# A graph layer and a top-1 mixture of experts on one core: the choice of the expert in two parts, the second layer's weight halves side by side, and the first routing rows loaded behind the border

## The chip, the core and the metric

The kernel runs on one core of a Trainium2 chip. TensorE (PE) multiplies matrices, VectorE (DVE), ScalarE (ACT) and GpSimd (POOL) work on rows in SBUF and on the banks (PSUM) that PE writes, and SyncE (SP) issues transfers. The metric is the device time of one execution in microseconds, lower is better.

## The reference

```python
x = x + graph_layer(layernorm(x), edges)         # 20000 rows of 256, 10000 edges
h = layernorm(x)
logits = h @ gate_w + gate_b                     # 8 experts
probs = softmax(logits); idx = argmax(probs)     # one expert for each row, ties to the first
kept = (rank of the row within its expert) < 3125   # at most 3125 rows each
hid = relu(h @ w1[idx] + b1[idx])                # 256 -> 1024
y = (hid @ w2[idx] + b2[idx]) * prob * kept      # 1024 -> 256
x = x + nan_to_num(y, posinf=1e4, neginf=-1e4)
```

In the graph layer each edge takes the normalised row of its sender, is weighted by a small network of its embedding (8 to 64 to 320) and by its direction, and is summed at its receiver. The sum goes through two 64x64 matrices and is added to the receiver's row. Everything is float32.

## The kernel before

The work is cut into four blocks of code, with a border (all engines wait for each other) between them. Each block has its own program for each engine, and the engines wait for one another by semaphores. The order within an engine is written out by hand.

**Edges and nodes, `edge_block`, 0 to 354 us.** There are 20 edge groups and 20 node chunks of eight tiles (40 transfers, 24 through `xin` and 16 through `shared`). The loop over steps g makes the radial weights (`ps_w`) and the messages of edge group g, and sums them per receiver (`ps_agg`, then the two matrices). ACT's order in a step is `rows_by_direction`, `take_agg`, `take_upd`, with the adding and storing of node chunks (`add_own_rows`, `store_rows`) woven in for the first STEPS = 10 steps. POOL gathers the senders' rows, works out scales (`node_scales`, `edge_scales`) and at the end adds the summed rows to DRAM (`scatter`). In the last steps, SP already loads the first four groups of new rows from `out` into `shared`, and DVE takes their layer statistics (`Early`, U = 4 buffers).

**Routing, `routing_block`, 354.8 to 527 us.** The 20480 rows (160 tiles of 128, the last few padding) go by in NG = 40 groups of four tiles. For each group PE turns the rows (16 transposes), ACT rounds them to a short format (`xt_hi`), DVE forms the rest (`xt_lo`, L1265) and, one group ahead, the statistics. PE then multiplies by the gate's weights and turns the logits back. POOL makes the coefficients of eight tiles (`coefs`) and the scaled logits (`scaled_logits`), 20 times each. After the last of them DVE chooses the expert of all 160 tiles in five operations from `best` (L1291) on:

```python
v.wait_ge(scaled_ready, NCO)
chain.link(red(best[:], logits[:], AX.X, ALU.max))
```

Then the places within each expert are counted, and tables of row numbers per expert are made.

**Experts, `expert_block`, 529 us to the end.** Rows of one expert are worked on in blocks, and each expert has some narrow blocks of two tiles first (its loop from `start` to `wide`), then wide ones of three tiles (from `wide` to `end`). Here there are 52 blocks, 14 narrow and 38 wide. A float32 product is made of three products of a short format: with a = a_hi + a_lo and b = b_hi + b_lo it is a_hi b_hi + a_lo b_hi + a_hi b_lo. For one block b:

- PE: the first layer (L1717) in eight parts f of 128 hidden units, six matmuls each over all the block's rows, into one of SLOTS = 4 banks `ps_h`. Then the second layer (L1729) in four parts j of two f each, for each tile and each f three matmuls of 256 columns into `ps_y`. After part 0 it turns the rows of block b + 1 into `ps_x` (L1707). The next f may start once the bank of f - 4 has been read (`h_taken`).
- ACT: the relu of each f twice, rounded (`h_hi`) and in full (`h_all`). Behind f == 1 it scales block b - 1's result by the probability (`scale_rows`, three activations), behind f == 3 it normalises the gathered rows of the block after next (`normalise`, L1641, 3 activations) and keeps their probabilities. Behind f == 7 it rounds the turned rows of b + 1 to `x_hi` (L1650). In the first wide block of an expert it also rounds four parts of the next expert's weights.
- DVE: `h_lo` in four parts, `x_lo`, the other four of the eight rounded weight parts and all eight low parts, `y_sum` (bank plus bias), and the clean-up of infinities.
- POOL: for b + 2 three pairs of gathers (`xg` L1462, `sg` L1468) also where the block has two tiles, then three adds of result rows into `out` (L1579). One loop runs over all blocks.
- SP: the loads of the next expert's weights.

The end, after the last block, scales and stores tile by tile (`scale_rows_end`, L1601), behind the whole second layer.

The rounded weights of both layers lie in one tile, the rest in another. The second layer's loop is, in short:

```python
for i in range(tiles):
    for f in (2 * j, 2 * j + 1):
        # h_hi x w_hi, h_lo x w_hi, h_hi x w_lo, 256 columns each
```

## Time and profile before

| | |
|---|---|
| median of 3 runs | 1412.29 us (1410.97 to 1415.54) |
| the profiled execution | 1410.77 us |
| its span, first to last instruction | 1408.9 us |
| busy: PE, DVE, ACT, POOL | 1213.6, 1001.1, 954.3, 1015.8 us |
| share of the span | 86%, 71%, 68%, 72% |
| mean granted clock of TensorE | 0.944 |

The busy times are those of one profiled execution. The share of an engine is an average over four stages with different limits, so the stages have to be read one by one. What a stretch waits for is seen in the chain that ended last, and in the bracket behind a row of the timeline: the idle time before that instruction, and what released it.

### The profile page before, as it was taken

What the parts mean: (1) busy time and instruction counts of PE and PEld (TensorE: products, weight loads), DVE (VectorE), ACT (ScalarE), POOL (GpSimd) and SP (SyncE); (2) the same over time, 40 slices, a digit from 0 to 9 for tenths busy, and PEclk for the clock granted to TensorE, in tenths of its full rate; (3) what the DMA queues carried; (4) which work ended last, traced back from release to release, by engine and by line L of the source; (5) the groups of instructions that cost most, each with busy time, mean ns of one, the idle gap of its engine ahead of it and who ended that gap; (6) DMA issues with size and microseconds to landing.
All of it is one profiled execution on the core that took longest, in us unless ns stands there. A gap on an engine that the chain in (4) does not pass through costs nothing.

```text
span 1408.9 us, 26705 instructions
## 1 busy us (share of the span) xinstructions
PE 1213.6 (86%) x7869; PEld 1067.7 (76%) x7870; DVE 1001.1 (71%) x2059; ACT 954.3 (68%) x2127; POOL 1015.8 (72%) x913
## 2 busy tenths in 40 slices
PE   2487578887998147999999999999999999999995
PEld 0244345555555137999999999999999999999995
DVE  7999998987898976657657555755755575556754
ACT  4789898885666256666667666766766776656673
POOL 7788878887788016767768767777776777678874
PEclk9977778999999588999999999999999999999998
DMA  9888996456776003433435323433423353333333
GB/s 336 235 269 280 289 213 163 70 85 110 218 219 225 9 8 98 109 45 46 109 46 114 50 45 46 109 47 50 109 45 45 49 114 47 45 46 53 54 54 40
DMA packets 131809, 153.01 MB, mean 109 GB/s; under 512 B 17218, under 2 KB 118658, under 8 KB 131606
## 3 DMA queue, kind: packets, MB, share of 16 engines
q0 software_dynamic: 51328, 64.07, 29.0%
q1 hardware_dynamic: 58758, 66.60, 14.7%
q10 hardware_dynamic: 21648, 21.49, 4.5%
q8 instruction: 29, 0.48, 0.1%
q14 instruction: 46, 0.38, 0.1%
HBM read 98.30 MB, written 53.81 MB: 108 GB/s over the span
## 4 chain that ended last, share of the span: by engine, by line
PE 57%; issue 2%; ACT 1%; POOL 1%; DMA 1%; DVE 1%; ACTq 0%; POOLq 0%; DVEq 0%
PE f_ps_y L1729 28%; PE f_ps_h L1717 26%; PE f_ps_x L1707 2%; DMA sg<-stat_rows,idx_now 1%; ACT y_all L1667 0%; ACT h_hi L1656 0%; ACT h_all L1657 0%; POOL xg L1462 0%; POOL sg L1468 0%; ACT f_xn L1641 0%; POOL out L1601 0%; DVE clean_end L1844 0%; DVE clean_end L1843 0%; ACT f_xn L1618 0%; DVE y_sum L1824 0%
## 5 line engine op out<-in xcount | busy, mean ns | idle before, releaser
L1656 ACT ACTIVATE h_hi<-f_ps_h,c_b 128x384 fp32r<-128x384 f32 (+1 forms) x416 | 236.4, 568 | 267.1 <-PE f_ps_h L1717 267.1
L1767 DVE TENSOR_TENSOR h_lo<-h_all,h_hi 128x768 fp32r<-128x768 f32 (+1 forms) x208 | 184.4, 886 | 258.3 <-ACT h_all L1657 257.1
L1729 PE MATMUL f_ps_y<-w_hi,h_hi 128*128 128x256 f32 x1136 | 325.4, 286 | 0.0
L1729 PE MATMUL f_ps_y<-w_hi,h_lo 128*128 128x256 f32 x1136 | 320.6, 282 | 0.0
L1729 PE MATMUL f_ps_y<-w_lo,h_hi 128*128 128x256 f32 x1136 | 319.1, 281 | 0.0
L1579 POOL DMA_INDIRECT out<-clean,put_now x156 | 255.8, 1640 | 56.7 <-issue 47.3
L1462 POOL DMA_INDIRECT xg<-out,idx_now x156 | 187.2, 1200 | 129.3 <-issue 120.6
L1717 PE MATMUL f_ps_h<-x_hi,w_hi 128*128 128x384 f32 (+1 forms) x832 | 271.3, 326 | 9.3 <-issue 3.4
L1717 PE MATMUL f_ps_h<-x_lo,w_hi 128*128 128x384 f32 (+1 forms) x832 | 268.6, 323 | 0.0
L1717 PE MATMUL f_ps_h<-x_hi,w_lo 128*128 128x384 f32 (+1 forms) x832 | 268.5, 323 | 0.0
L1657 ACT ACTIVATE h_all<-f_ps_h,c_b 128x384 f32<-128x384 f32 (+1 forms) x416 | 237.6, 571 | 0.0
L1468 POOL DMA_INDIRECT sg<-stat_rows,idx_now x156 | 189.7, 1216 | 47.9 <-issue 47.9
L1729 PEld LDWEIGHTS f_ps_y<-w_lo,h_hi 128*128 128x128 f32 x1136 | 215.3, 190 | 0.0
L1729 PEld LDWEIGHTS f_ps_y<-w_hi,h_hi 128*128 128x128 f32 x1136 | 213.3, 188 | 0.5 <-DVE h_lo L1767 0.3
L1729 PEld LDWEIGHTS f_ps_y<-w_hi,h_lo 128*128 128x128 f32 x1136 | 213.3, 188 | 0.0
L1717 PEld LDWEIGHTS f_ps_h<-x_hi,w_hi 128*128 128x128 f32 x832 | 157.7, 190 | 13.8 <-issue 8.4
L1717 PEld LDWEIGHTS f_ps_h<-x_lo,w_hi 128*128 128x128 f32 x832 | 157.9, 190 | 0.0
L1717 PEld LDWEIGHTS f_ps_h<-x_hi,w_lo 128*128 128x128 f32 x832 | 157.7, 190 | 0.0
L647 PEld LDWEIGHTS ps_agg<-same,msg 128*128 128x128 f32 x320 | 68.9, 233 | 66.2 <-issue 56.0
L647 PE MATMUL ps_agg<-same,msg 128*128 128x512 f32 (+3 forms) x320 | 114.6, 521 | 2.7 <-ACT late_rows L581 1.6
L636 PE MATMUL ps_w<-fc,hidden 64*128 64x320 f32 x160 | 59.8, 524 | 49.6 <-DVE tmp_h L808 48.8
L530 ACT ACTIVATE y<-y,edge_dir 128x256 f32<-128x256 f32 x240 | 100.0, 498 | 0.7
(245 smaller groups left out, 2260.8 us busy)
## 6 DMA issues: line engine op xcount, KB each, us to landing
shared<-out SPq DMA_DIRECT2D x40, 512.0 KB, 4.1
w_raw<-in_w SPq DMA_DIRECT2D x16, 1024.0 KB, 7.1
xin<-in_x SPq DMA_DIRECT2D x24, 512.0 KB, 7.2
out<-xin ACTq DMA_DIRECT2D x24, 512.0 KB, 5.5
shared<-in_x SPq DMA_DIRECT2D x16, 512.0 KB, 5.4
out<-shared ACTq DMA_DIRECT2D x16, 512.0 KB, 5.2
dst_row<-in_dst SPq DMA_DIRECT2D x20, 256.0 KB, 4.8
xg<-out,idx_now POOLq DMA_INDIRECT x156
```

Source lines behind the costliest of these rows:

```text
L530: ins = nc.scalar.activation(y[g % 2][:, t, 1 + i, :], y[g % 2][:, t, 0, :], ACT.Copy, scale=edge_dir[:, GT * g + t, i:i + 1])
L636: ins = nc.tensor.matmul(ps_w[:, t, :5 * MUL], hidden[:, t * P:(t + 1) * P], fc2[:], start=True, stop=True)
L647: ins = nc.tensor.matmul(ps_agg[:, c, t * P:], msg[g % 2][:, t].rearrange("p u j -> p (u j)")[:, c::2], same[g % 2][t][:], start=t == 0, s ...
L1462: return nc.gpsimd.indirect_dma_start(self.xg[:, i, :], None, self.out, bass.IndirectOffsetOnAxis(idx[:, i, 0:1].bitcast(U32), 0), bounds_ ...
L1468: return nc.gpsimd.indirect_dma_start(self.sg[:, i, :], None, self.stat_rows, bass.IndirectOffsetOnAxis(idx[:, i, 1:2].bitcast(U32), 0), b ...
L1579: nc.gpsimd.indirect_dma_start(out, bass.IndirectOffsetOnAxis(put_now[:, i:i + 1].bitcast(U32), 0), clean[:, i, :], None, bounds_check=ROW ...
L1656: nc.scalar.activation(h_hi[:, f, :n * P], ps_h[:, f % SLOTS, :n * P], ACT.Relu, bias=b1[:, e, f:f + 1])
L1657: nc.scalar.activation(h_all[f // 2 % 2][:, f % 2, :n * P], ps_h[:, f % SLOTS, :n * P], ACT.Relu, bias=b1[:, e, f:f + 1]).then_inc(h_taken, 1)
L1707: ins = nc.tensor.transpose(ps_x[:, c, i * P:(i + 1) * P], xn[:, i, c * P:(c + 1) * P], ident[:])
L1717: ins = nc.tensor.matmul(ps_h[:, f % SLOTS, :tiles * P], weights[s][:, w], x[:, c, :tiles * P], start=n == 0, stop=n == 5)
L1729: ins = nc.tensor.matmul(ps_y[:, i], x[:, f, i * P:(i + 1) * P], weights[s][:, w], start=i != 1 and f == 0 and n == 0, stop=f == KF - 1 an ...
L1767: tt(h_lo[:, pair, :n * P], h_all[j % 2][:, :, :n * P], h_hi[:, pair, :n * P].bitcast(F32), ALU.subtract).then_inc(h_lo_ready, 1)
```

## The change

- **Second layer.** The high and low halves of `w2` now lie side by side in one tile. `h_hi` is multiplied by both in one matmul of 512 columns, `h_lo` by the high half in one of 256. The bank `ps_y` is two halves wide for each tile (three banks), `ps_h` has three slots instead of four, and DVE adds both halves in two additions.
- **ACT and DVE.** Scaling by the probability moves from ACT to DVE. ACT rounds all weights (`AHEAD` = 6 parts before the relus, the rest behind `x_hi`), DVE forms only the low halves. `normalise` and `keep_prob` stand behind all eight relus. PE turns the next rows behind part 1 of the second layer instead of part 0.
- **POOL and SP.** POOL gathers two tiles for a narrow block; it has loops by expert for that, with a table `wide_blocks` that three more small DVE instructions make. SP waits for the gathers' landing and passes it on (`rows_in`), and issues the next expert's weight load at the start of each expert.
- **The last block** runs its second layer tile by tile, and DVE scales and cleans each tile as it is ready. The clearing of `y_sum` no longer stands before the first block.
- **The choice** of the expert is made for 144 tiles, once 18 of 20 parts of the logits are there, and then for the last 16.
- **Border.** `Early` goes: the first four groups are loaded after the border, SP's wait for the scatters written into the routing block, and their statistics are taken there.
- **Edge loop.** In ACT's program the adding of the last node chunk moves behind `rows_by_direction` and its store behind `take_upd`. The statistics of edge groups from 14 on are taken one step later and the coefficients of a step before its statistics. SP's loads of embeddings and receivers and POOL's `edge_scales` of one group come one place earlier.

```diff
+            next_receivers(STEPS - 1)
+            next_embedding(STEPS)
             for a in range(2):
                 sp.wait_ge(x1_out[(NC - 1) % RING][a], 16 * ((NC - 1) // RING + 1))
             sp.sem_inc(stored, 1)
-            next_receivers(STEPS - 1)
-            for g in range(STEPS, EG):
+            next_receivers(STEPS)
+            for g in range(STEPS + 1, EG):
...
-            for g in range(early.U):
-                early.load(sp, g)
...
-                if 2 * n - 2 < STEPS:
+                if 2 * n - 2 <= STEPS:
...
-                if g + 1 == STEPS:
-                    add_own_rows(2 * g + 1)
-                    store_rows(NC - 1, 1)
                 next_rows(g + 1)
                 rows_by_direction(g + 1, (0, 1))
                 take_agg(g - 1)
                 if g + 1 < STEPS:
                     add_own_rows(2 * g + 1)
                 rows_by_direction(g + 1, (2, 3))
+                if g + 1 == STEPS:
+                    add_own_rows(2 * g + 1)
                 take_upd(g - 1)
+            store_rows(NC - 1, 1)
...
-                return (n - 3) // 2 if n < STEPS else n - 6
+                if n >= SLOTS:
+                    return n - 5
+                return (n - 3) // 2 if n <= STEPS else n - 6
...
-            for g in range(U, NG):
-                sp.wait_ge(turned, g - U + 1)
-                sp.wait_ge(stats_ready, g - U + 1)
-                early.load(sp, g)
+            for g in range(NG):
+                if g >= U:
+                    sp.wait_ge(turned, g - U + 1)
+                    sp.wait_ge(stats_ready, g - U + 1)
+                if g % U == 0:
+                    needed = sp.value_load(writes.of_rows[0:1, g + U - 1:g + U], min_val=64,
+                                           max_val=32 * EG + 64)
+                    for h in range(2):
+                        sp.wait_ge(writes.scattered[h], needed)
+                        sp.sem_inc(spare_sp, 1)
+                sp.dma_start(rows[:, g % U], x1_v[g]).then_inc(rows_in[g % U], 16)
...
-            nc.vector.tensor_copy(stats[:, :U * GT], early.stats[:]).then_inc(stats_ready, U)
...
+            statistics(0)
             for g in range(NG):
-                if U <= g + 1 < NG:
-                    early.statistics(nc, v, g + 1, stats).then_inc(stats_ready, 1)
+                if g + 1 < NG:
+                    statistics(g + 1)
                 turned_half(g)
...
+            def choose(t):
+                n = t.stop - t.start
+                chain.link(red(best[:, t], logits[:, t], AX.X, ALU.max))
+                chain.link(tt(is_best[:, t], logits[:, t], over_experts(best[:, t]), ALU.is_equal))
+                chain.link(tt(score[:, t], is_best[:, t], falling_b[:].unsqueeze(1).broadcast_to([P, n, NEXP]), ALU.mult))
+                chain.link(red(first[:, t], score[:, t], AX.X, ALU.max))
+                chain.link(tt(chosen[:, t], score[:, t], over_experts(first[:, t]), ALU.is_equal))
+
+            LAST = 2 * CC
+            v.wait_ge(scaled_ready, NCO - 2)
+            choose(slice(0, NT - LAST))
             v.wait_ge(scaled_ready, NCO)
-            chain.link(red(best[:], logits[:], AX.X, ALU.max))
-            chain.link(tt(is_best[:], logits[:], over_experts(best[:]), ALU.is_equal))
-            chain.link(tt(score[:], is_best[:], over_tokens(falling_b), ALU.mult))
-            chain.link(red(first[:], score[:], AX.X, ALU.max))
-            chain.mark(tt(chosen[:], score[:], over_experts(first[:]), ALU.is_equal))
-            chain.wait()
+            choose(slice(NT - LAST, NT))
...
+            chain.mark(nc.vector.tensor_tensor_scan(wide_upto[:], ones_row[:, :NEXP], wide[:], 0.0, ALU.mult, ALU.add))
+            chain.mark(nc.vector.tensor_copy(wide_blocks[:, 0], wide[:1]))
+            chain.mark(tt(place[:], place[:], chosen[:], ALU.mult))
+            chain.wait(1)
+            chain.mark(stt(out=wide_blocks[:, 1], in0=wide_upto[:1], scalar=narrow[:1, 0:1], in1=wide[:1],
+                           op0=ALU.add, op1=ALU.subtract))
...
+        self.up_hi, self.up_lo, self.down = [], [], [[], []]
+        for n, up in enumerate((self.up_hi, self.up_hi, self.up_lo, self.up_lo)):
+            up.append(half(f"w_up{n}", [P, self.W1]))
+            self.down[n // 2].append(half(f"w_down{n}", [P, self.HALF, 2, D]))
...
-    SLOTS = 4
+    SLOTS = 3
+    AHEAD = 6
...
-        ps_y = ps("f_ps_y", [P, 4, D])
+        ps_y = ps("f_ps_y", [P, BT, 2, D])
...
+            def gather(b, tiles):
                 pool.wait_ge(idx_ready, b)
                 pool.sem_inc(spare_pool, 1)
-                for i in range(BT):
-                    gathers.rows(nc, idx_now, i).then_inc(gathered, 16)
-                    gathers.stats(nc, idx_now, i).then_inc(gathered, 16)
+                for i in range(tiles):
+                    landed = gathered if i < 2 else gathered_third
+                    gathers.rows(nc, idx_now, i).then_inc(landed, 16)
+                    gathers.stats(nc, idx_now, i).then_inc(landed, 16)
+
+            def step(b, tiles):
+                pool.wait_ge(xn_ready, b)
+                pool.wait_ge(prob_next_ready, b)
+                pool.sem_inc(spare_pool, 1)
+                gather(b, tiles)
+                add_rows(b - 3)
...
+                if split is not None:
+                    for c in range(AHEAD):
+                        weights.split_high(nc, act, e + 1, split, c)
...
-                    if f == 1:
-                        scale_rows(b - 1)
-                    if f == 3:
-                        act.wait_ge(turned, b + 1)
-                        act.sem_inc(spare_act, 1)
-                        normalise(b + 1)
-                        act.wait_ge(prob_ready, b + 2)
-                        act.sem_inc(spare_act, 1)
-                        keep_prob()
-                    if split is not None and f >= KF - BY_ACT:
-                        weights.split_high(nc, act, e + 1, split, f - (KF - BY_ACT))
+                act.wait_ge(turned, b + 1)
+                act.sem_inc(spare_act, 1)
+                normalise(b + 1)
+                act.wait_ge(prob_ready, b + 2)
+                act.sem_inc(spare_act, 1)
+                keep_prob()
                 take_high(b + 1)
+                if split is not None:
+                    for c in range(AHEAD, CUTS):
+                        weights.split_high(nc, act, e + 1, split, c)
...
-                pe.wait_ge(h_taken, KF * b + (f + 1))
+                pe.wait_ge(h_taken, KF * b + (f + 1 if f >= SLOTS else SLOTS))
...
+            def down(s, j, i):
+                for f in (2 * j, 2 * j + 1):
+                    w = w_down[s][f // HALF]
+                    nc.tensor.matmul(ps_y[:, i], h_hi[:, f, i * P:(i + 1) * P], w[:, f % HALF],
+                                     start=f == 0, stop=False)
+                    ins = nc.tensor.matmul(ps_y[:, i, 1], h_lo[:, f, i * P:(i + 1) * P], w[:, f % HALF, 0],
+                                           start=False, stop=f == KF - 1)
                 return ins
...
-                    if j == 0:
+                    hidden_ready(b, j)
+                    for i in range(tiles):
+                        ins = down(e % 2, j, i)
+                    if j == 1:
                         turn(b + 1)
                 ins.then_inc(y_ready, 1)
+
+            def last_step(e, b):
+                first_layer(e, b, BT)
+                for i in range(BT):
+                    for j in range(KJ):
+                        if i == 0:
+                            hidden_ready(b, j)
+                        ins = down(e % 2, j, i)
+                    ins.then_inc(y_tile_ready, 1)
...
+            def scale_rows(b):
+                v.wait_ge(y_sum_ready, b + 2)
+                v.wait_ge(prob_ready, b + 2)
+                v.wait_ge(clean_ready, b + 2)
+                v.sem_inc(spare_dve, 1)
+                tt(y_all[:], y_sum[:], prob[:].unsqueeze(2).broadcast_to([P, BT, D]), ALU.mult).then_inc(y_step, 2)
...
-                        for c in (2 * j, 2 * j + 1):
-                            if c < CUTS - BY_ACT:
-                                weights.split_own(nc, v, tt, e + 1, split, BY_ACT + c, (CUTS - BY_ACT) * e + c + 1)
-                            else:
-                                a = c - (CUTS - BY_ACT)
-                                weights.split_low(v, tt, e + 1, split, a, CUTS + BY_ACT * e + a + 1)
+                        for c in range(2 * j, min(2 * j + 2, AHEAD)):
+                            weights.split_low(v, tt, e + 1, split, c, CUTS * e + CUTS + c + 1)
...
-                tt(y_sum[:, :n], ps_y[:, :n], b2[:, bass.ds(e, 1)].broadcast_to([P, n, D]),
-                   ALU.add).then_inc(y_sum_ready, 1)
+                v.sem_inc(spare_dve, 1)
+                tt(y_sum[:, :n], ps_y[:, :n, 1], b2[:, bass.ds(e, 1)].broadcast_to([P, n, D]),
+                   ALU.add).then_inc(y_step, 1)
+                v.wait_ge(y_step, 3 * b + 3)
+                v.sem_inc(spare_dve, 1)
+                tt(y_sum[:, :n], ps_y[:, :n, 0], y_sum[:, :n], ALU.add).then_inc(y_sum_ready, 1)
...
+            add_infinities(last - 1)
+            keep_finite(last - 1)
+            nc.vector.tensor_copy(put_end[:], put_row[:, bass.ds(BT * last + 2 * BT, BT)])
+            v.wait_ge(prob_ready, last + 2)
+            v.wait_ge(clean_ready, last + 2)
+            v.sem_inc(spare_dve, 1)
             for i in range(BT):
-                v.wait_ge(y_end_ready, i + 1)
+                v.wait_ge(y_tile_ready, i + 1)
+                chain.link(tt(y_sum[:, i], ps_y[:, i, 1], b2[:, NEXP - 1], ALU.add))
+                chain.link(tt(y_sum[:, i], ps_y[:, i, 0], y_sum[:, i], ALU.add))
+                chain.link(ts(y_all[:, i], y_sum[:, i], prob[:, i:i + 1], None, ALU.mult))
```

## Rows read from the trace of the kernel before

**Rows 1.** Page part 4, the chain that ended last, by engine.

```profile
PE 57%; issue 2%; ACT 1%; POOL 1%; DMA 1%; DVE 1%; ACTq 0%; POOLq 0%; DVEq 0%
```

**Rows 2.** The chain in order of time, middle of the expert stage (start us, us, work).

```profile
587.35 8.33 PE f_ps_h L1717 x48
595.68 2.16 PE f_ps_y L1729 x18
...
598.50 6.47 PE f_ps_y L1729 x54
```

**Rows 3.** Table of stretches: busy us (instructions) of each engine, granted clock, DMA.

```profile
535.51:551.96 16.45, 15.36 (x103) 15.01 (x104) 6.11 (x11) 9.69 (x25) 7.26 (x8) 0.83 0.48 154
587.35:604.97 17.62, 17.62 (x127) 17.62 (x127) 9.38 (x13) 11.22 (x25) 12.86 (x10) 1.00 0.32 48
640.69:653.52 12.83, 12.64 (x103) 12.43 (x104) 7.15 (x13) 9.48 (x25) 8.62 (x7) 1.00 0.36 50
724.63:750.05 25.42, 25.00 (x205) 24.59 (x206) 14.68 (x25) 18.96 (x50) 18.73 (x15) 1.00 0.39 55
1256.38:1296.38 40.00, 38.06 (x307) 36.92 (x308) 22.51 (x38) 28.65 (x75) 30.59 (x23) 1.00 0.39 55
```

**Rows 4.** Timeline of PE in the routing block (start us, us, engine, line).

```profile
395.16 0.62 PE L1206 MATMUL banks<-xt_lo,r_gate_parts 128*8 128x512 f32 x2
395.62 0.60 PE L1193 MATMUL banks<-c_ident,shared 128*128 128x128 f32 x4
```

**Rows 5.** Timeline of ACT in the expert stage; brackets: idle before, releaser.

```profile
606.23 0.58 ACT L1656 ACTIVATE h_hi<-f_ps_h,c_b 128x384 fp32r<-128x384 f32 x1 [6.40 <-PE f_ps_h L1717]
...
611.28 1.61 ACT L1641 ACTIVATE f_xn<-xg,sg 128x256 f32<-128x256 f32 x3
...
616.57 0.87 ACT L1650 CAST x_hi<-f_ps_x 128x768 fp32r<-128x768 f32 x1
```

**Rows 6.** Timeline of POOL, same stretch.

```profile
596.38 1.09 POOL L1462 DMA_INDIRECT xg<-out,idx_now  x1 [2.27 <-issue]
...
605.74 1.63 POOL L1579 DMA_INDIRECT out<-clean,put_now  x1 [0.30 <-issue]
```

**Rows 7.** Timeline of POOL and ACT in the triple of narrow blocks.

```profile
1286.41 1.21 POOL L1468 DMA_INDIRECT sg<-stat_rows,idx_now  x1 [0.30 <-issue]
...
1289.21 0.20 ACT L1611 COPY idx_now<-idx_row 128x6 int32 x1 [2.06 <-DMA sg<-stat_rows,idx_now]
```

**Rows 8.** Timeline of ACT in the first expert block.

```profile
544.80 0.20 ACT L1611 COPY idx_now<-idx_row 128x6 int32 x1 [2.73 <-DMA sg<-stat_rows,idx_now]
```

**Rows 9.** The chain in order of time, the end.

```profile
1375.36 8.33 PE f_ps_h L1717 x48
...
1401.47 1.55 POOL out L1601
```

**Rows 10.** Timeline of DVE where the edge loop begins.

```profile
230.18 0.50 DVE L793 TENSOR_TENSOR tmp_d<-y 128x256 f32<-128x256 f32 x1 [5.61 <-PE ps_w L636]
```

**Rows 11.** Timeline of DVE and PE around the border (355 us).

```profile
342.83 5.31 DVE L157 BATCH_NORM_STATS2 early_stats<-shared 128x6 f32<-128x256 f32 x16
...
355.47 2.31 PEld L1193 LDWEIGHTS banks<-c_ident,shared 128*128 128x128 f32 x16
```

**Rows 12.** Page part 6, DMA issues: count, KB each, median us to landing.

```profile
shared<-out SPq DMA_DIRECT2D x40, 512.0 KB, 4.1
```

**Rows 13.** Timeline of DVE in routing and at the choice.

```profile
401.21 1.21 DVE L1265 TENSOR_TENSOR xt_lo<-banks,xt_hi 128x1024 fp32r<-128x1024 f32 x1
...
406.08 1.20 DVE L1265 TENSOR_TENSOR xt_lo<-banks,xt_hi 128x1024 fp32r<-128x1024 f32 x1
...
451.35 1.22 DVE L1265 TENSOR_TENSOR xt_lo<-banks,xt_hi 128x1024 fp32r<-128x1024 f32 x1 [0.21 <-ACT xt_hi L1147]
457.64 1.49 DVE L1291 TENSOR_REDUCE best<-logits 128x160 f32<-128x1280 f32 x1 [5.07 <-POOL logits L1112]
...
464.62 0.19 DVE L1297 TENSOR_TENSOR chosen<-chosen,c_valid 128x32 bf16<-128x32 bf16 x1
```

305 lines of the change are left out of this document (155 added, 150 removed).

## The prediction

> **What bounds the kernel now.** I read the page's chain first. TensorE carries 57% of it, nearly all in the two expert layers [rows 1]. So the next view is the chain in order of time in the middle of the expert stage. A block of three tiles costs 8.33 us for 48 first-layer matmuls, 2.16 and 6.47 us for 72 second-layer ones, and the rest of its 17.62 us is the turning of the next rows, 0.66 us [rows 2]. Nothing is idle in it. The table of stretches says the same: PE busy for 17.62 of 17.62 us, DVE 9.38, ACT 11.22, POOL 12.86, at a granted clock of 1.00 [rows 3]. Blocks of two tiles are different. Their PE work is 48 and 48 matmuls of 256 columns and one turn. At 6.47/54 = 0.1198 us each that is 11.50 + 0.66 = 12.16 us. They take 12.83 us alone, 25.42 as a pair, and 40.00 us as a triple [rows 3]. So a few tenths are lost in each and 3.5 us in the triple. There are 38 wide and 14 narrow blocks: one narrow at the start, two alone, four pairs, one triple. Before the expert stage stand the edge loop, where ACT, PE and DVE take turns, and routing, where DVE and POOL are both full.
>
> **The second layer.** Per tile and hidden chunk, three matmuls of 256 columns become one of 512 and one of 256. Columns are equal, instructions go from three to two. What is an instruction worth? 384 columns take 8.33/48 = 0.1735 us and 256 take 0.1198 [rows 2]. The difference, 0.0537 for 128 columns, is 0.42 ns each, which is the 2.4 GHz level, and leaves 0.1198 - 0.1074 = 12.4 ns that do not depend on columns. A 512-column matmul would then take 0.2272 us and replace 0.2396: 12.4 ns saved. The only fast-format 512-column matmuls in the trace are the gate's. Two of them start at 395.16 and the next work at 395.62, 0.23 us each [rows 4]. That is 10 ns saved, but their weights are 8 columns wide. The bounds are 0 (the row says nothing of 128 columns of weights; a loss has no reason, as the columns are the same) and 12.4. I take 12.4, since both shapes it is drawn from have this very weight load. With 24 merges in a wide block that is 0.30 us, over 37 blocks 11.1 us (the last one is counted at the end). A narrow block has 16, 0.20 us.
>
> The Trainium skill (TensorE: Matmul & The Clock Gate, "Wait — 56ns, not 53.3ns?") gives the warm spacing as columns over 2.4 GHz plus about 2.5 ns. By that the 1136 merges would save 2.8 us and not 14.1. This trace has five times that constant in both shapes, so the row decides.
>
> **What ACT and DVE exchange.** Scaling by the probability (three ACT activations) goes to DVE as one product of 768 elements, priced as its neighbours of that size, some 0.95 us. The sum of the second layer takes two DVE additions instead of one, another 0.95. DVE rises from 9.4 to 11.3 us of 17.3 in a wide block, and has nothing behind it that PE needs early: the new sum has the whole first layer to finish in. All weight highs go to ACT. That is 4 more casts of 0.6 us, six of them ahead of the relus. In the block before, ACT's last work is x_hi, which is done 3 us before the block ends, so these six (3.1 us) fill an idle stretch. DVE loses its own four. Zero for both; if the cover goes, about 1 us in each of seven blocks.
>
> **ACT's order.** Now scaling stands behind the second relu and normalising behind the fourth, and with four slots PE overruns them in narrow blocks. Afterwards the eight relus run through. The third slot lost costs nothing, since a relu pair is faster than PE's six matmuls for it in a wide block and equal in a narrow one. So a narrow block can fall to its PE work, 12.16 - 0.20 = 11.96 us.
>
> But normalising comes later. In a wide block the relus begin 1.26 us in [rows 2, 5]. From 606.23 to 616.57 are 10.34 us, of which scaling and normalising take 2.9 [rows 5]. So relus end 8.7 us in, the rows are normalised at 10.4 (now 7.9), and the next gather begins at 11.5 (now 596.38 - 587.35 = 9.0) [rows 2, 6]. Six gathers take 605.74 - 596.38 = 9.36 us, and landing about 1.6 more (1287.62 to 1289.21) [rows 6, 7]. They land 5 us into the next block and are wanted at 8.7. Turning moved behind the second part of the second layer, at 12.5 us, so PE is safe by another 2. Wide blocks lose nothing. The relay through SP adds some 0.2.
>
> **Narrow blocks.** POOL now gathers two tiles, 4 instructions instead of 6, so 9.36 falls to some 6 us, and its 15.1 us per block no longer exceed the block. This is what ran dry in the triple: ACT waits 2.06 us for the gather there [rows 7]. A narrow block followed by anything but a narrow one keeps its pace: 12.83 to 11.96, twice, gives 1.7 us. In a pair, the gather of the following wide block can start only when the second narrow block's rows are normalised, 9.3 us into the first. It takes 8.2 to 9.4, lands 1.6 to 2.4 later, and is wanted at 8.5 of the second. The turn comes 0.9 to 2.2 us late; I take 1.5. A pair is then 23.9 + 1.5 = 25.4, as now, four times 0. The triple is 35.9 + 1.5 = 37.4, a gain of 2.6. Together 4.3 us; the bounds are 0.7 (2.2 us of stall each) and 7.2.
>
> **The first block** takes 16.45 us [rows 3]. ACT stands before the first gather's landing with four relus behind it (2.73 us idle, to 544.80) [rows 8]. Afterwards the relus have run and the second layer's first two parts too when the rows land. PE's first layer ends as now at about 543.7. With 5.55 + 0.66 it ends at some 549.9, plus 0.5 for a start that no longer waits for POOL's memset: 2.4 us gained, between 0 and 4.
>
> **The end.** From the last first layer (1375.36) to POOL's last add (1403.02) are 27.66 us [rows 9]. Now the adds of the last block but one wait until the next x_lo is through; afterwards DVE forms them right behind the last hidden part, at 12.1 us. Three adds then end at 18.5. The tiles finish at 11.1, 13.9 and 16.7, each with 2.8 us of DVE work, so POOL adds them until 23.9. 3.8 us gained; bounds 2 and 5.
>
> **The edge loop.** DVE waits 5.61 us for ps_w at 230.18 [rows 10], because ACT has put both halves of the last node chunks ahead of the edge rows. Moving the last chunk behind them starts the loop earlier, but the update that frees PE's bank still stands behind it. I take 1.7 us, bounds 0 and 5.6. The statistics moved by one step lie in DVE's idle parts; scatters start one statistics (1.8 us) later, and POOL idles before the border anyway. SP's two early loads only come sooner.
>
> **The border and the choice.** Now the first four row groups are in SBUF and their 16 statistics done (from 342.83, while DVE would wait), and PE turns at 355.5 [rows 11]. Afterwards SP issues the load after the border, 4.1 us to landing [rows 12]. DVE must do all 40 groups at (406.08 - 401.21)/2 = 2.44 us [rows 13]. The first low half comes at 362.2 instead of 357.7, the last ends at 457.3 instead of 452.6, and POOL's last logits come at about 460.4 instead of 457.6. The choice takes 464.62 - 457.64 = 6.98 us now, after POOL's last logits [rows 13]. In two parts: 144 tiles, nine tenths and the fixed parts, 6.4 us, from 457.3 to 463.7; 16 tiles, five small instructions of 0.3, to 465.2. That is 0.6 later than now, and the three small instructions for wide_blocks add 0.5. Sum +1.1; bounds -1 and +5 (the four loads share one queue).
>
> **Sum.** -11.1 - 4.3 - 2.4 - 3.8 - 1.7 + 1.1 = -22.2 us. The profiled execution took 1410.8, so 1388.6; the median of the runs is 1.5 above it, hence 1390.
>
> **Rivals.** A: the merged matmul takes the time of the two. For it: no 512-column row with full weights. Against: two shapes on one line, and the gate's 0.23. Price 14.1: 1404. The skill's constant, named above, is nearly this case: 11.3 us dearer, 1401. Chance for both 0.12.
> B: gathers are late in narrow blocks, and the border costs its upper bound. Stalls of 3 us in each of five groups and 4 us at the border: +7.5 + 4, 1402. For it: DVE's longer work of two inputs beside POOL's gathers. Chance 0.13.
> C, slower: the gather chain of every wide block becomes the bound. Its slack is 3.7 us at ACT and 2.1 at PE. To turn 22 us of gain into a loss of 4 needs 0.5 us in each of 51 blocks, thus gathers that land 6.3 us later than worked out. Time 1416 and more. Against it: six gathers never took more than 9.4 us in the middle of the stage. Chance 0.07.
> D: the gains hold and the stalls in pairs are small, edge loop at its bound: -7.2 instead of -4.3 and 3 more at the edge, 1384. Chance 0.18.
> The forecast itself, 1385 to 1395: 0.50.
>
> **Range and chances.** 1381 to 1403 takes in the forecast, B, D and half of A. A measurement of this kernel tells about 0.3%, 4 us. Faster 0.87 (all but C, and A and B together), same 0.06, slower 0.07.
>
> **What would show it.** In the profile after: a wide block's period of 17.3 us with 24 + 24 second-layer matmuls in 8.3; if it is 17.6, the first step is wrong. Narrow pairs of 25.4 with one wait of ACT for sg in the second; POOL with 4 gathers there. DVE's last low half at about 455.6 (with the edge gain), the big choice right behind it, and POOL's logits no longer in front of the choice. POOL's last add some 24 us after the last block's start. Wrong it would be made by a wait of PE on f_xn in wide blocks, or by 512-column matmuls spaced 0.24 us.

## The result, and the profile after

The changed kernel takes 1402.8 us (median of 5 runs, 1400.08 to 1406.13) against 1412.29 (5 runs, 1410.97 to 1416.48). The ratio is 0.9932, 95% interval 0.9913 to 0.9951. It is faster, by 9.5 us where 22 were forecast. One execution of all that follow, of early_and_sixth_relu, was slow (1785.3 us at a mean granted clock of 0.65, where the others of that kernel have 0.94 to 0.95); it is left out everywhere. The profiled execution took 1401.79 us with a span of 1400.0, against 1410.77 and 1408.9.

The table of stretches shows the first block, a wide block, a single narrow block, a pair, the triple, and a late wide block, to be read against [rows 3]:

```profile
536.27:551.28 15.01, 14.32 (x87) 13.31 (x88) 6.90 (x12) 10.68 (x26) 5.80 (x6) 0.85 0.52 167
604.02:621.61 17.59, 17.59 (x104) 16.49 (x103) 10.62 (x15) 10.69 (x22) 12.94 (x10) 1.00 0.62 164
639.19:652.29 13.10, 12.44 (x88) 11.25 (x87) 8.68 (x14) 10.41 (x26) 10.36 (x8) 1.00 0.35 52
722.62:748.82 26.20, 24.64 (x174) 22.45 (x173) 17.09 (x27) 18.91 (x48) 18.74 (x14) 1.00 0.32 43
1253.08:1290.62 37.54, 36.80 (x261) 33.64 (x259) 26.23 (x43) 27.28 (x70) 27.86 (x21) 1.00 0.34 47
1166.08:1183.48 17.40, 17.40 (x104) 16.32 (x103) 11.07 (x15) 10.62 (x22) 12.85 (x10) 1.00 0.31 53
```

PE does 24 instructions less in a wide block, and the block takes 17.59 us instead of 17.62. Single narrow blocks and pairs have become longer, 13.10 for 12.83 and 26.20 for 25.42. They have by more than that: the narrow stretches of [rows 3] end where the chain enters the next block (653.52), and that block's first matmul starts 0.16 us earlier (653.36). From first matmul to first matmul, as the stretches here are cut, the kernel before took 12.67 and 25.25, and 39.84 for the triple. Only the first block and the triple are shorter. The late wide block takes 17.40, with the same work at the same granted clock. The chain in order of time shows where those two differ, to be read against [rows 2]:

```profile
604.19 8.48 PE f_ps_h L1741 x48
...
1166.24 8.33 PE f_ps_h L1741 x48
```

The first layer, which the change does not touch, takes 8.48 us for its 48 matmuls in most blocks of the changed kernel, 176.7 ns each, and 8.33 in the last ones, 173.5 ns each as before.

Below, a layer's time is the difference between two starts in PE's timeline. The first matmul of the first layer of block 0 and that of the last block bound the expert stage. All of the time that was gained or lost in us, by that reckoning (minus is shorter; forecast are the terms of the sum as they stood):

| part | forecast | profiled |
|---|---|---|
| 37 wide blocks: second layer and turn | -11.1 | -10.4 |
| 37 wide blocks: first layer | 0 | +3.5 |
| two single narrow blocks | -1.7 | +0.7 |
| four pairs | 0 | +3.7 |
| the triple | -2.6 | -2.3 |
| the first block | -2.4 | -1.3 |
| the end | -3.8 | -3.7 |
| edge loop, border, choice | -0.6 | +0.8 |
| sum | -22.2 | -9.0 |

Of the 10.4 us in the first line, 4.5 are not the matmuls' own. Before, PE stood still for 0.64 us at each of the seven changes from a wide block to the next expert; the timeline of PE in the kernel before shows the gap behind the last second-layer matmul:

```profile
639.93 0.28 PE L1729 MATMUL f_ps_y<-w_hi,h_lo 128*128 128x256 f32 x1
640.69 0.38 PE L1717 MATMUL f_ps_h<-x_hi,w_hi 128*128 128x256 f32 x1 [0.47 <-issue]
```

Nothing released that matmul but PE's own sequencer. In the changed kernel there is no such row. In PE's program the three bounds of the next expert's loops are read from SBUF (`value_load`) at just this place, between the wide loop of one expert and the narrow loop of the next; between an expert's narrow and wide loop nothing is read, and PE does not stop there in either kernel. A merge itself took 0.19 us off the second layer of a wide block (9.29 to 9.10), 8 ns for each of 24. With 37 blocks that is 7.0 us; 1.2 us were lost again in the wide blocks behind the triple and behind three of the pairs, whose rows were turned 0.05 to 0.5 us late. The latest, in PE's timeline:

```profile
1303.74 0.87 PE L1731 MATMUL f_ps_x<-c_ident,f_xn 128*128 128x128 f32 x6 [0.34 <-ACT f_xn L1669]
```

A narrow block behind a wide one, in the timelines of DVE and ACT, the turn in PE's, and a row of ACT's in the next block:

```profile
726.26 0.69 DVE L1809 TENSOR_TENSOR h_lo<-h_all,h_hi 128x512 fp32r<-128x512 f32 x1 [1.27 <-ACT h_all L1685]
...
728.90 0.47 ACT L1684 ACTIVATE h_hi<-f_ps_h,c_b 128x256 fp32r<-128x256 f32 x1 [0.25 <-DVE h_lo L1809]
...
730.43 1.60 ACT L1669 ACTIVATE f_xn<-xg,sg 128x256 f32<-128x256 f32 x3
...
732.08 0.88 PE L1731 MATMUL f_ps_x<-c_ident,f_xn 128*128 128x128 f32 x6 [0.30 <-ACT f_xn L1669]
...
743.57 0.20 ACT L1649 COPY idx_now<-idx_row 128x6 int32 x1 [0.96 <-SPq L1590]
```

The block began at 722.62. The relus end 7.7 us in, the rows are normalised at 9.4, and PE turns them at 9.5. PE itself would have been there at 6.17 + 8 x 0.352 = 9.0 with the first layer as it is, and at 5.75 (48 x 0.1198) + 2.81 = 8.56 with one that never waits for a slot; both are estimates from these rows. The last row belongs to the second narrow block of the pair: there ACT waits for the gather (through SP), 0.96 us. The chain of the triple and of the pairs runs through ACT's f_xn each time.

In routing, a row of PE's timeline answers to [rows 11], and one of DVE's, the first low half, to [rows 13]:

```profile
357.56 3.68 PE L1178 MATMUL banks<-c_ident,shared 128*128 128x128 f32 x16 [3.21 <-DMA shared<-out]
...
360.61 1.23 DVE L1256 TENSOR_TENSOR xt_lo<-banks,xt_hi 128x1024 fp32r<-128x1024 f32 x1 [0.18 <-ACT xt_hi L1132]
```

PE waits 3.21 us for the first rows, and its turn takes 3.68 instead of 2.6. At the choice, in DVE's timeline:

```profile
457.33 1.34 DVE L1280 TENSOR_REDUCE best<-logits 128x144 f32<-128x1152 f32 x1
...
463.75 0.29 DVE L1280 TENSOR_REDUCE best<-logits 128x16 f32<-128x128 f32 x1
...
465.33 0.19 DVE L1291 TENSOR_TENSOR chosen<-chosen,c_valid 128x32 bf16<-128x32 bf16 x1
```

The big choice takes 6.42 us and the small one 1.58, as worked out (6.4 and 1.5), right behind DVE's last low half. The border comes 1.7 us earlier, and the choice ends 0.7 later all the same.

### The profile page after: what moved, and what is told of

Read it like the earlier page. It is cut to its first block, busy times and chain, and to the rows that moved or that the text cites. A ratio compares the mean times of both kernels' runs of the same rounds, so it can differ in the third digit from the quotient of the medians.

```text
span 1400.0 us, 24873 instructions
## 1 busy us (share of the span) xinstructions
PE 1213.1 (87%) x6728; PEld 1008.9 (72%) x6728; DVE 1068.9 (76%) x2150; ACT 928.5 (66%) x1990; POOL 989.2 (71%) x881
## 4 chain that ended last, share of the span: by engine, by line
PE 44%; issue 5%; POOL 3%; DVE 3%; ACT 2%; DMA 2%; DVEq 1%; POOLq 0%; ACTq 0%; SPq 0%
PE f_ps_h L1741 20%; PE f_ps_y L1753 14%; PE f_ps_y L1755 7%; PE f_ps_x L1731 2%; POOL out L1612 2%; DMA out<-clean,put_now 1%; ACT f_xn L1669 1%; POOL sg L1475 1%; DVE y_all L1817 1%; DMA sg<-stat_rows,idx_now 1%; DVE y_sum L1878 1%; DVE h_lo L1809 1%; DVE clean L1838 1%; DVE clean L1843 1%; POOL xg L1469 1%
## 5 line engine op out<-in xcount | busy, mean ns | idle before, releaser
L1741 PE MATMUL f_ps_h<-x_hi,w_up 128*128 128x384 f32 (+1 forms) x1664 | 405.4, 325 | 5.3 <-DVE x_lo L1851 3.8
L1753 PE MATMUL f_ps_y<-w_down,h_hi 128*128 128x512 f32 x1136 | 408.3, 399 | 0.1
L1755 PE MATMUL f_ps_y<-w_down,h_lo 128*128 128x256 f32 x1136 | 318.4, 280 | 0.0
L1741 PEld LDWEIGHTS f_ps_h<-x_hi,w_up 128*128 128x128 f32 x1664 | 294.0, 189 | 10.0 <-issue 4.2
L1741 PE MATMUL f_ps_h<-x_lo,w_up 128*128 128x384 f32 (+1 forms) x832 | 269.9, 324 | 0.0
L1753 PEld LDWEIGHTS f_ps_y<-w_down,h_hi 128*128 128x128 f32 x1136 | 213.4, 188 | 47.4 <-DVE h_lo L1809 0.5
L1755 PEld LDWEIGHTS f_ps_y<-w_down,h_lo 128*128 128x128 f32 x1136 | 213.8, 188 | 0.0
L1804 DVE TENSOR_TENSOR x_lo<-f_ps_x,x_hi 128x768 fp32r<-128x768 f32 x51 | 48.8, 957 | 148.2 <-ACT x_hi L1678 148.2
L1741 PEld LDWEIGHTS f_ps_h<-x_lo,w_up 128*128 128x128 f32 x832 | 157.7, 190 | 0.0
L125 POOL DMA_INDIRECT out<-rows,upd_row x48 | 86.8, 1809 | 29.3 <-DMA out<-rows,upd_row 17.1
```

The source lines that it names most:

```text
L1741: ins = nc.tensor.matmul(ps_h[:, f % SLOTS, :tiles * P], weights[s][:, w], x[:, c, :tiles * P], start=n == 0, stop=n == 5)
L1753: nc.tensor.matmul(ps_y[:, i], h_hi[:, f, i * P:(i + 1) * P], w[:, f % HALF], start=f == 0, stop=False)
L1755: ins = nc.tensor.matmul(ps_y[:, i, 1], h_lo[:, f, i * P:(i + 1) * P], w[:, f % HALF, 0], start=False, stop=f == KF - 1)
```

## The experiments

Each kernel below was run beside the kernel before on the same chip; that kernel's medians there were 1411.87 to 1412.80. "Stage" is the expert stage, "slow" how many of the 37 wide blocks have a first layer above 8.44 us (in nine kernels one of these is long by a single late matmul), "border" the start of POOL's first instruction behind it, "choice" the time from DVE's first instruction there to the start of its first work that is no longer part of the choice (`below`). All are of the one profiled execution; what is blank was not counted, since first layers wait for ACT there.

| kernel | median (runs) | stage | slow | border | choice |
|---|---|---|---|---|---|
| before | 1412.29 (5) | 839.7 | 4 | 354.8 | 109.8 |
| changed | 1402.80 (5) | 833.7 | 28 | 353.1 | 111.9 |
| changed_again | 1400.69 (4) | 832.2 | 22 | 352.9 | 112.7 |
| second_layer_split | 1408.79 (10) | 837.0 | 2 | 356.7 | 114.0 |
| merge_alone | 1505.95 (4) | | | 352.8 | 109.9 |
| normalise_early_in_narrow | 1420.93 (5) | 851.5 | 32 | 352.8 | 112.9 |
| normalise_behind_sixth_relu | 1395.73 (4) | 825.5 | 31 | 359.8 | 111.8 |
| three_tiles_gathered | 1409.40 (10) | 837.5 | 21 | 361.9 | 112.4 |
| early_rows_restored | 1397.68 (4) | 829.6 | 6 | 357.6 | 107.4 |
| choice_in_one_part | 1407.55 (10) | 833.3 | 24 | 356.0 | 115.6 |
| edge_order_undone | 1403.62 (6) | 832.6 | 28 | 354.4 | 113.6 |
| early_and_sixth_relu | 1384.35 (5) | 819.6 | 4 | 353.1 | 106.7 |
| early_and_sixth_relu_again | 1386.03 (5) | 819.0 | 7 | 359.9 | 107.0 |
| both_and_old_edge_order | 1388.13 (5) | 820.8 | 5 | 357.8 | 106.7 |
| last_part_in_256 | 1389.17 (5) | 824.3 | 2 | 353.2 | 106.6 |
| bounds_one_expert_ahead | 1392.30 (6) | 823.9 | | 354.4 | 107.5 |
| moved_384_bytes | 1399.92 (7) | 829.9 | 7 | 358.8 | 112.3 |
| moved_128_bytes | 1400.96 (10) | 829.0 | 7 | 355.6 | 112.0 |
| moved_320_bytes | 1404.53 (10) | 833.8 | 37 | 354.6 | 113.8 |
| best_moved_128_bytes | 1387.91 (4) | 821.6 | 15 | 356.0 | 107.0 |

### What is a merge worth, and at what price

**second_layer_split**: the changed kernel with

```diff
-                    nc.tensor.matmul(ps_y[:, i], h_hi[:, f, i * P:(i + 1) * P], w[:, f % HALF],
-                                     start=f == 0, stop=False)
+                    for low in range(2):
+                        nc.tensor.matmul(ps_y[:, i, low], h_hi[:, f, i * P:(i + 1) * P], w[:, f % HALF, low],
+                                         start=f == 0 and low == 0, stop=False)
```

> The changed kernel, but the second layer as three matmuls of 256 columns again; layout, slots and everything else as changed. Measured so far: in the changed kernel the second layer and turn of a wide block take 9.10 us instead of 9.29, and the first layer 8.48 instead of 8.33 in 28 of 37 blocks. Theory 1 (a merge saves some 8 ns, and the mixed stream of 512 and 256 columns is what leaves the first layer in its slower spacing): second layer back to 9.29, first layer back to 8.33, wide blocks 17.62, the whole 1.5 us slower than the changed kernel or less. Theory 2 (the first layer's spacing has another cause, the layout or the slots): first layer stays at 8.48, wide blocks 17.77, and the whole is 37 x 0.19 = 7 us slower.

The second layer is back at 9.29 us and the first at 8.33 in 35 blocks, as theory 1 has it. But the stage is 3.4 us longer than with merges, not 1.5, because the stop at the change of expert is back in all seven places (a second layer of 9.93 us). PE's timeline has it as before:

```profile
729.30 0.38 PE L1741 MATMUL f_ps_h<-x_hi,w_up 128*128 128x256 f32 x1 [0.48 <-issue]
```

So the merges gave 11.1 us in the second layer of the 37 wide blocks (348.9 to 337.8), 4.5 of them at the changes, and lost 3.8 in their first layer and 4.0 in the 14 narrow blocks, which get their rows no earlier when PE does not stop ahead of them. Whether the stop comes with the columns or with the number of instructions ahead of the bounds' reading, this run can't tell: both change together.

**merge_alone**: the kernel before with the merged second layer, three slots and two additions, and ACT's old order.

```diff
-    SLOTS = 4
+    SLOTS = 3
...
-        ps_y = ps("f_ps_y", [P, 4, D])
+        ps_y = ps("f_ps_y", [P, BT, 2, D])
```

> The kernel before with the second layer of the change alone: weight halves side by side, 512 and 256 columns, three slots for the first layer's banks, two additions for y_sum. ACT still scales behind the second relu and normalises behind the fourth. Theory 1 (with three slots the order of ACT has to change too): PE wants the bank of part 4 for part 7 at 7.3 us of a wide block and gets it at 9.0, wide blocks 18.5 to 19.2 us instead of 17.62, narrow ones 13.9 or more, the whole 40 to 80 us slower than before. Theory 2 (the third slot costs nothing even in the old order): wide blocks 17.40 to 17.58, the whole 5 to 12 us faster than before.

It is 93 us slower than before (ratio 1.0666, 1.0634 to 1.0698), more than expected. A wide block takes 19.44 us: the second layer and turn 9.07, the first layer 10.37. PE's waits from 550 to 1400 us (in total, times, longest):

```profile
PE f_ps_h L1731 <- ACT h_all L1671: 75.7, 92, 1.4
```

And in PE's timeline of one block:

```profile
558.88 0.45 PE L1731 MATMUL f_ps_h<-x_hi,w_up 128*128 128x384 f32 x1 [0.22 <-ACT h_all L1671]
562.42 0.45 PE L1731 MATMUL f_ps_h<-x_hi,w_up 128*128 128x384 f32 x1 [1.18 <-ACT h_all L1671]
```

The bank that the merge needs for `ps_y` is taken from `ps_h`, and with ACT's scaling and normalising between the relus three slots do not cover it. Theory 1 holds. Moving them out from between the first relus is what makes the merge pay.

**last_part_in_256**: early_and_sixth_relu (below), the wide matmul split in two for the last of four parts, `if j == KJ - 1`.

> As early_and_sixth_relu, but in the last of the four parts of the second layer the wide matmul is two of 256 columns again, 6 of 24 merges in a wide block. Theory 1 (a stretch of 256-column matmuls ahead of the first layer brings its spacing back to 173.5 ns, as in the kernel with all of them split, where 35 of 37 first layers took 8.33 us): nearly all first layers 8.33, second layer 9.07 + 6 x 0.009 = 9.12, wide blocks 17.45, 1 to 4 us faster than early_and_sixth_relu. Theory 2 (the share of merged matmuls or the layout decides): first layers at 8.48 in about as many blocks, and 2 us slower by the lost merges.

Slow first layers fell from 4 to 2, so it had nothing to win there, and it is 4.8 us slower: the second layer of the seven last wide blocks is 9.8 us, with PE's stop at the change of expert back. Six merges split right ahead of the change are enough to bring it back; the eighteen before them do not help.

### Why the first layer became slower

The new spacing was gone in early_rows_restored as well, which touches no matmul. There the early statistics' tile of 384 bytes lies ahead of all the tensors of the expert stage. Four kernels move the tensors alone:

```diff
         writes = Writes(ctx, nc)
+        ctx.enter_context(nc.sbuf_tensor("pad", [P, 96], F32))      # 384 bytes; 32 and 80 for 128 and 320
```

> The changed kernel with an unused SBUF tensor of 384 bytes per partition ahead of the routing and expert tensors, which puts the weights and rows where they lie with the early statistics restored. Theory 1 (where the tensors lie decides the first layer's spacing, once the second layer is merged: 20 to 32 of 37 first layers took 8.48 us at the changed kernel's addresses in five kernels, 4 or 5 in three kernels with the early statistics' 384 bytes ahead): at most 8 first layers at 8.48, wide blocks 17.40, 3 us faster than the changed kernel. Theory 2 (something else of those kernels, their order before the border): 20 or more at 8.48.

> As moved_384_bytes with 128 bytes. Under theory 1 the number of slow first layers may be that of either class, and tells which multiple matters: 384 and 128 are equal modulo 256. If it is low here and there, the place modulo 256 decides; if it is low only with 384, a coarser one; if high in both, theory 2.

> As moved_384_bytes with 320 bytes, which puts the weights at the very addresses of the kernel before. Theory 1: a number of slow first layers that is set by this place, 8 or fewer if multiples of 128 or more decide. Theory 2: 20 or more at 8.48, as in the changed kernel.

> early_and_sixth_relu with 128 unused bytes more, which is the changed kernel's place modulo 256 again. Theory 1 with a period of 256 bytes: 20 or more first layers at 8.48 instead of 4, wide blocks 17.58, the whole 3 us slower than 1384. Theory 2: still 3 to 8 at 8.48.

With 384 and 128 bytes 7 blocks are slow, with 320 all 37. The chain of moved_320_bytes, two blocks:

```profile
571.29 8.48 PE f_ps_h L1741 x48
588.88 8.48 PE f_ps_h L1741 x48
```

The same of moved_128_bytes:

```profile
571.15 8.33 PE f_ps_h L1741 x48
588.55 8.33 PE f_ps_h L1741 x48
```

Theory 1 holds: with the merged stream, the place of the tensors in SBUF decides how often. The stage is 829.0 and 829.9 against 832.2 to 833.8. Count the shift from the changed kernel modulo 256 bytes: at 128 (384 and 128) seven kernels have 2 to 7 slow blocks, at 0 eight have 15 to 32, at 64 (320) one has 37. The best kernel moved by 128 is shifted by 512, at 0 again, and has 15. That fits a period of 256 bytes, but one kernel at 64 does not prove it. At 0 the state differs from one execution to the next (28 and 22 blocks for the same program) and mostly holds for all of an expert's wide blocks; at 128 every slow block is an expert's first (30 of 38) or second (8), and the next is fast again. The tensors of merge_alone and moved_320_bytes lie where the kernel before has them, and that one, with 256 columns in the whole second layer, has 4 slow blocks. So it takes both, the mixed stream and the place. In medians of runs the effect of 3 us can't be told from the differences between runs.

### Narrow blocks

**normalise_early_in_narrow** and **normalise_behind_sixth_relu**: the changed kernel with

```diff
                 for f in range(KF):
                     relu(e, b, f, n)
-                act.wait_ge(turned, b + 1)
...
-                keep_prob()
+                    if f == (3 if n == 2 else KF - 1):      # 5 in the other kernel
+                        act.wait_ge(turned, b + 1)
...
+                        keep_prob()
```

> The changed kernel, but in blocks of two tiles ACT normalises behind the fourth relu, as before the change. Theory 1 (the turn of a narrow block is late because normalising now stands behind eight relus that need 7.7 us): PE no longer waits for f_xn in narrow blocks, each of them falls from 12.98 to between 12.0 and 12.6, the whole 3 to 10 us faster. Theory 2 (the gathered rows land late, so where ACT normalises does not matter): ACT waits for the gather behind the fourth relu with four relus queued behind it, narrow blocks stay at 12.98 or become longer.

> The changed kernel, but in blocks of two tiles ACT normalises behind the sixth relu of eight. Theory 1 (in the changed kernel the turn is 0.9 us late because ACT normalises behind all relus; behind the fourth PE runs out of its three slots instead): with the sixth both fit, the relus of parts 6 and 7 are done before the last part of the second layer wants them, narrow blocks fall from 12.98 to 12.0 to 12.3, those that wait for their gather stay at 13.2, and the whole is 4 to 7 us faster. Theory 2 (any normalising between relus makes PE wait for a slot): first layer of narrow blocks longer than 6.2 us, no gain or a loss.

Behind the fourth relu, the turn is no longer late: second layer and turn of the pairs take 6.27 us, their matmuls' own time. But the first layer takes 7.60, with one row in PE's timeline that says why:

```profile
737.12 0.39 PE L1742 MATMUL f_ps_h<-x_hi,w_up 128*128 128x256 f32 x1 [1.64 <-ACT h_all L1685]
```

The block takes 13.87 us, the single ones 16.20 and 14.63, and the first one 19.81, because ACT meets its gather with four relus behind it. So theory 1 has the lateness of the turn right and the cure wrong, and the whole is 20 us slower than changed_again. Behind the sixth relu both fit. The pair takes 24.63 us instead of 26.20:

```profile
727.75:752.38 24.63, 24.43 (x174) 22.58 (x173) 17.16 (x28) 18.53 (x48) 18.97 (x14) 1.00 0.34 46
```

The stage falls to 825.5 us with 31 slow first layers, 6.7 to 8.1 less than the changed kernel, and the median is 5.0 below changed_again. Theory 1 holds. The second block of a pair, which the expectation left at 13.2, fell too: ACT still waits 1.10 us for its gather there, but the gather starts 8.7 us into the first block instead of 10.5, so PE no longer waits for the rows in any narrow block.

**three_tiles_gathered**: POOL's loop of narrow blocks with `step(b, BT)`, and one loop of SP for all blocks.

> The changed kernel, but POOL gathers three tiles for every block again, and one loop of SP passes the landing on. Theory 1 (two tiles instead of three shorten POOL's chain where narrow blocks follow each other): single narrow blocks stay at 12.98, the third block of the triple goes from 12.4 back to some 14, pairs lose 0.3 to 1 us each, the whole 3 to 6 us slower. Theory 2 (POOL was never late but in the triple): only the triple changes, by 2 us.

Single narrow blocks are the same (26.1 for two), the pairs take 106.7 us in place of 104.6 in all, the triple 40.1 in place of 37.5. So some 4.6 us in the stage, the size that theory 1 has, but not its shape: two of the four pairs became shorter (25.5 us), one took 26.8 and one 28.9, where PE waits 2.0 us for the rows. With one execution profiled, the 4.6 is of that execution. The rest of the 8.7 us in the median is not of this stage.

**bounds_one_expert_ahead**: early_and_sixth_relu with

```diff
+            ahead = bounds(v, 0)
             for e in range(NEXP):
-                start, wide, end = bounds(v, e)
+                start, wide, end = ahead
                 with v.Fori(start, wide) as b:
                     step(e, b, 2)
                 if e + 1 < NEXP:
+                    ahead = bounds(v, e + 1)
                     step(e, wide, BT, 1 - e % 2)
```

and the same for ACT.

> early_and_sixth_relu, but ACT and DVE read an expert's first, first wide and last block from their table one expert earlier. In the first narrow block of an expert the first layer takes 6.17 us and 5.70 in the second of a pair; there DVE's first h_lo begins 1.0 us after ACT's second h_all has ended, and in the second of a pair 0.1 us after it. Theory 1 (DVE reads the table between the blocks, and the late h_lo delays ACT and PE's slots): h_lo right behind h_all, first layer 5.75, seven experts times 0.4: 3 us faster. Theory 2 (the two additions of y_sum over three tiles are what makes DVE late): 6.17 stays, no difference.

DVE's first h_lo of the narrow block, in the timeline of early_and_sixth_relu:

```profile
718.06 0.69 DVE L1828 TENSOR_TENSOR h_lo<-h_all,h_hi 128x512 fp32r<-128x512 f32 x1 [1.26 <-ACT h_all L1703]
```

And of bounds_one_expert_ahead:

```profile
720.04 0.69 DVE L1830 TENSOR_TENSOR h_lo<-h_all,h_hi 128x512 fp32r<-128x512 f32 x1 [0.31 <-ACT h_all L1703]
```

It comes 0.95 us sooner, and the stretch of the pair and of the wide block behind it shows both sides:

```profile
717.36:741.34 23.98, 23.98 (x174) 22.49 (x173) 17.61 (x27) 17.74 (x46) 18.73 (x14) 1.00 0.37 55
741.34:760.37 19.03, 18.21 (x105) 16.21 (x103) 16.02 (x25) 13.63 (x29) 14.70 (x11) 1.00 0.30 50
```

Narrow blocks are at 12.0 us, PE never idle: theory 1's mechanism is right. But now the same reading stands in front of the first wide block, where ACT and DVE also round the next expert's weights, and that block takes 18.0 to 19.1 us in six of the eight experts. PE's own reading of the bounds was left where it is, so this run says nothing of PE's stop. The stage is 4.3 to 4.9 us longer, and the median 6.3 above early_and_sixth_relu_again.

### Border, choice and edge loop

**early_rows_restored**: class `Early` back, its loads at the end of SP's edge program, its statistics at the end of DVE's, and `statistics(g)` out of routing for the first four groups.

```diff
+            for g in range(early.U):
+                early.load(sp, g)
...
-            statistics(0)
             for g in range(NG):
-                if g + 1 < NG:
-                    statistics(g + 1)
+                if U <= g + 1 < NG:
+                    early.statistics(nc, v, g + 1, stats).then_inc(stats_ready, 1)
```

> The changed kernel, but the first four row groups are loaded and their statistics taken before the border, as before the change. Theory 1 (removing them cost DVE 4.8 us of a stretch that the choice no longer waits beyond): the last xt_lo ends some 98 us after the border's end instead of 104, the choice in two parts ends some 4 us earlier, and the whole is 3 to 4 us faster, the border itself 0.75 us later. Theory 2 (POOL's logits were the bound, as in the kernel before): xt_lo ends earlier but the choice waits for POOL, gain under 1 us.

DVE's last low half ends 99.0 us behind DVE's first instruction instead of 103.8 to 105.9, and the choice ends at 107.4 instead of 111.8 to 114.0. Its border came at 357.6, but in other kernels with the early rows at 352.8 to 359.9, and without them at 352.8 to 361.9. Theory 1 holds: some 5 us of work came back onto DVE's path.

**choice_in_one_part**:

```diff
-            v.wait_ge(scaled_ready, NCO - 2)
-            choose(slice(0, NT - LAST))
             v.wait_ge(scaled_ready, NCO)
-            choose(slice(NT - LAST, NT))
+            choose(slice(0, NT))
```

> The changed kernel, but the expert of all 160 tiles is chosen in one part once all logits are there. Theory 1 (POOL's last logits end after DVE's last xt_lo at 457.4 as they did before, by 3 to 5 us): DVE idles for that long and the choice ends 2 to 4 us later than 465.3. Theory 2 (with DVE's later finish POOL is not behind any more): the choice starts at 457.5, takes 7.0 us and ends at 464.6, under 1 us earlier than in two parts.

POOL's last logits come 3.9 us behind DVE's last low half, the choice starts there and ends 11.0 us behind that half, against 8.0 in two parts: the two parts are worth 3.0 us here. With the early rows POOL is 6.8 us behind (early_and_sixth_relu, 104.5 against 97.7), and they are worth some 5 (POOL's 104.5 and a choice of 7.1 would end at 111.6 instead of 106.7).

**edge_order_undone** and **both_and_old_edge_order**: the edge loop of before in ACT's, DVE's, SP's and POOL's programs, in the changed kernel and in early_and_sixth_relu.

> The changed kernel with the edge loop of before: the last node chunk ahead of the edge rows, statistics and coefficients in their old steps, SP's and POOL's early items back. So far the border began 7.68 us after POOL's last scatter in seven of ten kernels, among them the one before, and 0.3 us after ACT's last copy in the other three, and it moved between 352.8 and 361.9 us with the same code. Theory 1 (POOL's scatters set the border, so the order of ACT and DVE in the loop gains nothing): no difference of the medians beyond 2 us. Theory 2 (the new order gains the 1.7 us that were predicted): 1 to 3 us slower than the changed kernel's 1401 to 1403.

> As early_and_sixth_relu, and the edge loop of before as well. If the new order of the edge loop is worth nothing, the same time within 2 us; if it is worth the predicted 1.7, slower by that; if it makes POOL's scatters start later and so moves the border, faster by 1 to 4 us.

In the first pair the medians are 1403.6 and 1402.8 or 1400.7, in the second 1388.1 and 1384.4 or 1386.0. One thing is clear: DVE's long wait for ps_w [rows 10] stands in all four traces of the old order (5.6 to 8.2 us) and in none of the sixteen of the new one. But PE starts ps_w of edge group 11 as long behind that of group 8 in the changed kernel as in the one before, 52.9 us (others: 50.8 to 52.8 in the new order, 53.2 to 58.6 in the old). All differences point to a gain of the new order of 1 to 4 us, none is clear of the spread, and the two views of a run can't settle it, because of what sets the border. POOL's timeline of three_tiles_gathered:

```profile
352.70 1.55 POOL L125 DMA_INDIRECT out<-xin,upd_row  x1 [0.30 <-issue]
361.92 0.10 POOL L1100 MEMSET power<- 128x8 f32 x1 [7.68 <-POOLq L178]
```

The border ends 7.68 us behind POOL's last scatter there, as in the kernel before (347.12 and 354.80) and ten of the others; in the remaining eight, the changed kernel's own trace among them, it ends 0.3 us behind ACT's last copy, with POOL waiting up to 10.6. POOL's last scatter ended anywhere between 342.2 and 354.2 with the same order of work.

### Together

**early_and_sixth_relu**, and the same again:

> The changed kernel with the first four row groups loaded and measured before the border again and, in blocks of two tiles, normalising behind the sixth relu. Each alone gave 1397.7 and 1395.7 against 1400.7 and 1402.8 for the changed kernel. If the two gains are independent, 1390 to 1393. If the stretch before the border eats the first (border 4 us later, since DVE's statistics wait for POOL's scatters), 1395.

> early_and_sixth_relu unaltered, beside the kernel above on the same chip. 1384 within 3 us, and again at most 8 of 37 first layers at 8.48 us if the place of the tensors sets that number.

1384.4 us, ratio 0.9803 (0.9785 to 0.9821), and 1386.0, ratio 0.9802 (0.9775 to 0.9829). That is the best version, 15 to 18 us below the changed kernel, where the two gains by themselves would give 8 to 12. The stage is 819.6, of which a part is the place of the tensors:

```profile
580.18:597.58 17.40, 17.40 (x104) 16.32 (x103) 11.07 (x16) 10.63 (x22) 12.83 (x10) 1.00 0.30 46
714.43:739.09 24.66, 24.47 (x174) 22.50 (x173) 17.16 (x27) 18.52 (x48) 19.02 (x14) 1.00 0.33 47
```

**changed_again**:

> The changed kernel once more, unaltered, for comparison with the others on this chip. If the first layer's spacing of 176.7 or 173.5 ns (8.48 or 8.33 us in a wide block) is a state that the stream falls into by chance, another number than 28 of 37 wide blocks takes 8.48 us. If it is fixed by the program, it is the same 28 blocks. The stretch before the border differed by up to 4 us between kernels with the same code there, and does so again.

1400.69 us, 22 slow blocks and not the same ones.

## Why the prediction was right and wrong

The time lies just inside the range (1381 to 1403) and on the side that had 0.87, but of the 22 us only 9.5 came. That it is inside is luck: without the 4.5 us of PE's stops, which nobody had in the sum, it would be at 1407. The steps, in its own order:

**"I take 12.4, since both shapes it is drawn from have this very weight load."** Mis-sized. A merge took 8 ns off, as PE's spacing for 512 and 256 columns together is 0.3517 us (9.10 - 0.66 over 24) where 0.347 was worked out. The straight line through two shapes did not reach to the third. The gate's pair, 10 ns, was nearer. By the constant of about 2.5 ns that the Trainium skill (TensorE: Matmul & The Clock Gate, "Wait — 56ns, not 53.3ns?") adds to columns over 2.4 GHz, a merge would save an estimated 2.5 ns; 8 were measured, so here it is too small.

**That the first layer keeps its 8.33 us** was not even written down as a step, and it failed: +3.5 us, shown to depend on the merged stream together with the place of the tensors. That the merges remove PE's stop of 0.64 us at seven changes, -4.5 us, was missed too: the narrow stretches of [rows 3] begin behind the stop, and the 2% of issue in [rows 1] were left without a cause. The two nearly cancel, which made the wide blocks' 6.9 us look like a smaller merge and nothing else.

**"So a narrow block can fall to its PE work, 12.16 - 0.20 = 11.96 us."** This step failed, and it is the largest: 13.10, 26.20 and 37.54 us instead of 11.96, 25.4 and 37.4. The prediction had both numbers in its passage on pairs: rows normalised 9.3 us into a narrow block, turned at 8.5. It set the first against the next block's gather alone, and did not see that their difference is a wait of PE in the same block; PE waits for f_xn in 12 of the 13 narrow blocks behind the first. Measured, the relus run until 7.7, the rows are there at 9.4 and the turn comes at 9.5. Besides, [rows 3] reads each narrow stretch 0.16 to 0.18 us too long, so 1.2 of the 4.3 us forecast for narrow blocks were not there to be gained. The kernel that normalises behind the sixth relu brought 7.9 us back (6.0 of them in the pairs), and with the table's reading moved the blocks took 12.0, the floor that was forecast. What was said of the gather in a pair, 0.9 to 2.2 us late, came out, PE waits 0.9 to 1.0 us there and ACT 0.96 for the gather; but the cause was again ACT's order, as the kernel with the sixth relu shows, where the same gather starts 1.8 us sooner and PE does not wait. Two gathered tiles are worth 4.6 us, and the triple gained 2.3 of the forecast 2.6.

**"The third slot lost costs nothing, since a relu pair is faster than PE's six matmuls."** True only behind the new order of ACT, and just so: in wide blocks hardly a wait appears, with the old order PE waits 92 times between 550 and 1400 us. In the first narrow block of an expert PE waits about 0.2 us for a slot, as before with four.

**What ACT and DVE exchange, "Zero for both".** In wide blocks this held: DVE is busy 11.1 us of 17.4. In a narrow block the product stands between the first two h_lo, and a relu waits 0.25 us for the second.

**The first block**, 2.4 us, gave 1.3, and between 1.3 and 2.5 in the other kernels with the same code; ACT took up the gathered rows 9.75 us into the block (546.02), against 9.29 before [rows 8]. **The end**, 3.8 us, gave 3.7: right.

**"The edge loop. I take 1.7 us ... POOL idles before the border anyway."** The reason given was wrong: in the kernel before the border came 7.68 us behind POOL's last scatter, and it does so in twelve of the twenty traces, while ACT's last copy lies 1 to 8.5 us ahead of it; POOL set the end there. DVE's wait did go, but whether the 1.7 us were there can't be told. **Border and choice**, forecast 0.6 us later than before, and 0.5 for the small instructions: the choice ends 2.0 to 4.2 us later, counted from DVE's first instruction (which itself starts 0.36 us later behind the border than before), and nothing shows of the 0.5. In the changed kernel's own trace the first low half starts 7.5 us behind the border, as worked out (7.4), but the last ends 1.9 later than forecast: 362.2 + 39 x 2.44 is the start of the last half and not its end, which is 1.2 us short. In the ten other kernels that load these rows behind the border the first low half starts 9.0 to 10.7 us behind it. Restoring the early rows gives it all back.

Of the rivals, B came nearest in time and partly in cause: stalls in narrow blocks, though by ACT's order and only in the pairs by the gather, and a border above its forecast. That B's 1402 was hit is luck. A's price was partly paid too. C did not occur, but its slack was smaller than written: relus were taken to end 8.7 us into a wide block, and the last pair can't start before PE ends part 8 at 8.33. In ACT's timeline of the block at 1183.48 the rows are normalised from 9.7 to 11.3 instead of until 10.4, and PE turns them at 12.5:

```profile
1193.15 1.59 ACT L1669 ACTIVATE f_xn<-xg,sg 128x256 f32<-128x256 f32 x3
```

The wide blocks behind the triple and three pairs used this up.

## What to carry to other kernels

When work is moved behind a series on an engine, make the sum of when its result is wanted for the shortest block, not for the commonest one; here the longest block had 1.3 us to spare and the shortest lacked 0.9. When a stage's instructions get fewer or wider, compare also the stages that were not touched, and the places where loops end: the gain and the loss there were each as large as half of the direct effect. A buffer taken from one stage for another has to be tried with the order that was built around it: alone it cost 93 us.

## What the runs showed of the hardware

The same 48 matmuls of 384 columns take 8.33 or 8.48 us, at a granted clock of 1.00 in both cases. With 256-column matmuls before them they nearly always take 8.33 (35 and 33 of 37 blocks). With 512 and 256 columns in turn it depends on where the tensors lie: 2 to 7 slow blocks of 37, 15 to 32, or all of them, for shifts of 0 to 512 bytes. Why was not found.

PE stops for 0.64 us where it goes from the wide loop of one expert to the narrow loop of the next, if the last matmuls have 256 columns, and not behind the stream with 512 columns. Eighteen 256-column matmuls behind eighteen merges of the same block are enough to bring the stop back. Where it goes from an expert's narrow loop to its wide one it never stops, whatever the columns. What differs in the program is the reading of the loop bounds from SBUF, which stands only at the first of these places; no run moved it in PE's program, so that it causes the stop is argued and not shown.
